# A decoder layer on one core: self-attention scores in two 64-row halves, a new order of TensorE's work, and gathers moved back in the first stage

## The chip, the cores and the metric

One core of a Trainium2 chip runs the whole program, with full-precision (f32) data. The metric is the time of one execution in microseconds (us) on the device. Engines: TensorE (PE; its weight loads are listed as PEld), VectorE (DVE), ScalarE (ACT), GpSimd (POOL) and SyncE (SP), which issues most DMAs.

## What is computed

`x` has 32 sequences of 64 tokens, 512 wide. The layer adds a self-attention, a cross-attention and a linear layer with low-rank additions, each on the layer norm of `x`:

```python
x = x + self_attention(layernorm(x), w_q, w_k, w_v, w_o)          # 32 heads of 16
x = x + cross_attention(layernorm(x), ctx, ctx, positions, mask)   # 32 heads of 128, 8 key/value heads, rotary
x = x + linear_with_lora(layernorm(x))
# self-attention, per head: softmax(q @ k.T / 4) @ v
# keys of the cross-attention: k = ctx @ Wk, then k * cos[pos] + rotate_half(k) * sin[pos]
```

## The kernel before

Five stages follow each other, each with its own buffers and a barrier between them: keys and values of the cross-attention (`keys_and_values`), layer norm and self-attention values (`norm_and_values`), `self_attention`, `cross_attention`, `lora_linear`. In each stage every engine has its own list of instructions, written out by hand in program order; semaphores tie them together. A product of two f32 matrices is made of three fp32r matmuls over high and low parts (`product3`, lines 75 to 77: the first, second and third).

**Self-attention** runs 16 iterations `it`: 4 groups of 8 heads (128 of the 512 columns) by 4 blocks of 512 tokens (8 sequences). In each iteration TensorE projects q and k (`project`, 12 matmuls of 128x512 each), ScalarE spreads them out with zeroed heads (`spread_q` 2 copies, `spread_k` 4 copies, lines 415 and 423), and then 4 units of 2 sequences each go through `scores` (line 349; one f32 matmul a sequence over all 128 rows, 128 queries wide and 256 keys deep), `shift` on VectorE (maximum and subtraction, lines 476 and 479), `exponentials` on ScalarE (430), `invert` on VectorE (sum and reciprocal, 484 and 487), `normalise_p` on GpSimd (552), `turn` on TensorE (4 transposes, 358), `copy_turned` on ScalarE (435) and `mix` with the values (373; the output in four groups of 32 columns). The result of an iteration is split (`outputs_hi` 440, `outputs_lo` 491), multiplied by `w_o` (`output`, 6 matmuls for two tiles of tokens) and added to x (`add`, 509); the last group also collects norm statistics in `add` (line 122). `place_values` (501) lays out the values of the next iteration with 4 VectorE copies.

TensorE's order in unit n is: scores(n+2), mix(n-1), turn(n), and then one of project k, output, project q, output. The buffers of scores, probabilities and their sums are double.

**Keys and values** of the cross-attention: SP loads the context and `wv` chunk by chunk, then `wk`; GpSimd issues 16 gathers of table rows (line 674) as soon as the positions are there. TensorE first makes the 8 value tiles of block 0 one after the other, transposes the gathered rows into cosine and sine tables (814), and then makes the keys of block 0; blocks 1 to 3 alternate keys and values. Each key tile is rotated by three VectorE operations into `ra` and `rb` (563 to 565), which GpSimd adds into `k_out` (681), and SP stores that. `rotate` of a tile waits for the addition of the tile before it, since `ra` and `rb` are single. `keys` of a tile waits until the tile two before it has been rotated.

Of the kernel before, what the change touches and what calls it, by code (L numbers as in the profile page):

```python
# [26 lines left out]
P = 128  # L27
# [12 lines left out]
QSETS, KSETS = 2, 4  # L40
# [217 lines left out]
def self_attention(nc, stack_type, x, norm2, xt_hi, xt_lo, v1, ident, wq_dram, wk_dram, wo_dram, heads_dram):  # L258

    with stack_type() as stack:  # L260
# [3 lines left out]
        UNITS, UB = 4, BLOCK // SEQ // 4  # L264
        UNITS_ALL = ITS * UNITS
        BB = BLOCK // SEQ
        raw = {w: m.sb(f"raw_{w}", [P, KC, P]) for w in "qk"}
# [4 lines left out]
        heads = m.sb("heads", [P, QSETS + KSETS])  # L272
        q_x = [m.sb(f"q_x{i}", [P, BB, QSETS, SEQ]) for i in range(2)]
        k_x = [m.sb(f"k_x{i}", [P, BB, KSETS, SEQ]) for i in range(2)]
# [3 lines left out]
        pn = [m.sb(f"pn{i}", [P, UB * KSETS, SEQ]) for i in range(2)]  # L278
        pt = [m.sb(f"pt{i}", [P, UB * KSETS // 2, P]) for i in range(2)]
        mx = [m.sb(f"mx{i}", [P, UB * KSETS]) for i in range(2)]  # L280
        total = [m.sb(f"total{i}", [P, UB * KSETS]) for i in range(2)]
        inv = [m.sb(f"inv{i}", [P, UB * KSETS]) for i in range(2)]
        o_hi, o_lo = m.sb("o_hi", [P, BLOCK], F32R), m.sb("o_lo", [P, BLOCK], F32R)
        ps_in = {w: m.ps(f"ps_{w}") for w in "qk"}
        ps_o, ps_p = m.ps("ps_o"), m.ps("ps_p")
        ps_s = [m.ps(f"ps_s{i}") for i in range(2)]
# [9 lines left out]
        v_ready, pv_done, out_hi, out_lo, y_done, y_added = (m.sem(n) for n in ("v_ready", "pv_done", "out_hi", "out_lo", "y_done", "y_added"))  # L296

        block = stack.enter_context(nc.Block())

# [3 lines left out]
        def block_of(it):  # L303
            return it % NB

# [26 lines left out]
        def _(pe):  # L332
            def project(w, it):

                need(pe, ready[w], group_of(it) + 1)
                need(pe, {"q": q_spread, "k": k_spread}[w], it)
                tokens = slice(block_of(it) * BLOCK, (block_of(it) + 1) * BLOCK)
                product3(nc, ps_in[w][:, :], [(w_hi[w][:, c, :], w_lo[w][:, c, :], xt_hi[:, c, tokens], xt_lo[:, c, tokens])
                                           for c in range(KC)]).then_inc(done[w], 1)

            def scores(n):

                it, u = n // UNITS, n % UNITS
# [3 lines left out]
                for r in range(UB):  # L347
                    b = u * UB + r
                    mm = nc.tensor.matmul(ps_s[n % 2][:, r * KSETS * SEQ:(r + 1) * KSETS * SEQ],
                                          q_x[it % 2][:, b, :, :].rearrange("p e q -> p (e q)"),  # L350
                                          k_x[it % 2][:, b, :, :].rearrange("p j k -> p (j k)"), start=True, stop=True)
                mm.then_inc(s_done, 1)

            def turn(n):
                need(pe, p_norm, n + 1)
                need(pe, pt_copied, n)
                for i in range(UB * KSETS // 2):
                    tr = nc.tensor.transpose(ps_p[:, i * P:(i + 1) * P], pn[n % 2][:, 2 * i:2 * i + 2, :].rearrange("p j k -> p (j k)"),
                                             ident[:, :])
                tr.then_inc(p_turned, 1)  # L360

            def mix(n):

                it, u = n // UNITS, n % UNITS
                need(pe, pt_copied, n + 1)
                if u == 0:
                    need(pe, v_ready, it + 1)
                    need(pe, out_lo, it)
                for r in range(UB):
                    b = u * UB + r  # L370
                    for c in range(HPG1 // 2):
                        half, e = c % (KSETS // 2), c // (KSETS // 2)
                        mm = nc.tensor.matmul(ps_o[c * 2 * D1:(c + 1) * 2 * D1, b * SEQ:(b + 1) * SEQ], v_x[it % 2][:, b, c, :],
                                              pt[n % 2][:, r * KSETS // 2 + half, e * SEQ:(e + 1) * SEQ], start=True, stop=True)
                mm.then_inc(pv_done, 1)

            def output(it, pair):
                need(pe, out_lo, it + 1)
                need(pe, ready["o"], group_of(it) + 1)
                need(pe, y_added, it * 2 + pair)  # L380
                for t in (2 * pair, 2 * pair + 1):
                    product3(nc, ps_y[:, t % 2, :], [(o_hi[:, t * P:(t + 1) * P], o_lo[:, t * P:(t + 1) * P],
                                                      wo_hi[:, :], wo_lo[:, :])]).then_inc(y_done, 1)
# [4 lines left out]
            scores(0)  # L388
            scores(1)
            for n in range(UNITS_ALL):  # L390
                it, u = n // UNITS, n % UNITS
                if n + 2 < UNITS_ALL:
                    scores(n + 2)
                if n > 0:
                    mix(n - 1)
                turn(n)
                if u == 0 and it + 1 < ITS:
                    project("k", it + 1)
                if u == 1 and it > 0:
                    output(it - 1, 0)  # L400
                if u == 2 and it + 2 < ITS:
                    project("q", it + 2)
                if u == 3 and it > 0:
                    output(it - 1, 1)
            mix(UNITS_ALL - 1)
            output(ITS - 1, 0)
            output(ITS - 1, 1)

        @block.scalar
        def _(act):  # L410
            def spread_q(it):
                need(act, done["q"], it + 1)
                need(act, s_done, (it - 1) * UNITS)
                for e in range(QSETS):
                    c = nc.scalar.activation(q_x[it % 2][:, :, e, :], ps_in["q"][:, :].rearrange("p (b q) -> p b q", q=SEQ), ACT.Copy,
# [3 lines left out]
            def spread_k(it):  # L419
                need(act, done["k"], it + 1)  # L420
                need(act, s_done, (it - 1) * UNITS)
                for j in range(KSETS):
                    c = nc.scalar.activation(k_x[it % 2][:, :, j, :], ps_in["k"][:, :].rearrange("p (b q) -> p b q", q=SEQ), ACT.Copy,
                                             scale=heads[:, QSETS + j:QSETS + j + 1])
                c.then_inc(k_spread, 1)

            def exponentials(n):
                need(act, s_shifted, n + 1)
                need(act, p_norm, n - 1)
                nc.scalar.activation(p[n % 2][:, :, :], s[n % 2][:, :, :], ACT.Exp, scale=SCALE).then_inc(p_exp, 1)  # L430

            def copy_turned(n):
                need(act, p_turned, n + 1)
                need(act, pv_done, n - 1)
                nc.scalar.activation(pt[n % 2].rearrange("p i q -> p (i q)"), ps_p[:, :], ACT.Copy).then_inc(pt_copied, 1)

            def outputs_hi(it):
                need(act, pv_done, (it + 1) * UNITS)
# [10 lines left out]
            exponentials(0)  # L449
            exponentials(1)  # L450
            for n in range(UNITS_ALL):
                it, u = n // UNITS, n % UNITS
                if u == 1 and it + 1 < ITS:
                    spread_k(it + 1)
                if u == 3 and it + 2 < ITS:
                    spread_q(it + 2)
                if u == 0 and it > 0:
                    outputs_hi(it - 1)
                copy_turned(n)
                if n + 2 < UNITS_ALL:  # L460
                    exponentials(n + 2)
                if block_of(it) == NB - 3 and u == 3 and group_of(it) + 1 < G1:
                    split_hi(act, "q", group_of(it) + 1, done["q"], it + 3)
# [1102 lines left out]
```

## Time and profile before

| | |
|---|---|
| median of 3 runs | 1610.09 us (1608.79 to 1610.84) |
| the profiled execution's own time | 1609.72 us |
| its span, first to last instruction | 1607.8 us |
| busy, share of the span | PE 93%, PEld 74%, DVE 70%, ACT 29%, POOL 30% |
| mean granted TensorE clock | 0.972 |
| `keys_and_values` | 0 to about 209 us |
| `norm_and_values` | about 209 to 271 us |
| `self_attention` | about 271 to 552 us |
| `cross_attention` and `lora_linear` | from 552 us |

A row of the timeline gives the start, the duration from the first start to the last end, the engine, the line, the operation with its tiles, how many instructions were merged, and in brackets the idle time before it and what ended it.
### The profile page before, as it was taken

To read this page: it belongs to the slowest core of one execution; us is meant where nothing else is said; L and a number is where in the kernel's file an instruction comes from. 1 tells how busy PE (TensorE), PEld (TensorE's weight loads), DVE (VectorE), ACT (ScalarE), POOL (GpSimd) and SP (SyncE) were. 2 spreads that over 40 slices of the span, in tenths; PEclk is the share of its full clock that TensorE was granted. 3 is DMA by queue.
4 is the path that set the end of the run, shared out by engine and by line. 5 is a ranking of instruction groups with operands and counts; after the bars stand their busy time and mean duration, and the time that the engine had idled before them with its cause. 6 is when DMAs were issued, how large, how long until landed. Compare 5 with 4: busy or idle time off the path is not lost. (4 is left out here: it accounts for less than half of the span.)

```text
span 1607.8 us, 25367 instructions
## 1 busy us (share of the span) xinstructions
PE 1502.7 (93%) x9824; PEld 1192.1 (74%) x9824; DVE 1132.3 (70%) x1819; ACT 458.3 (29%) x802; POOL 481.1 (30%) x411
## 2 busy tenths in 40 slices
PE   7899978999999569999999999999999999998698
PEld 5688856677777357787778878877877787786476
DVE  3555333688888677787887787787887877886454
ACT  4111133565555221222221221222222212211311
POOL 4322212222222123332432423433333324231022
PEclk9999989999999779999999999999999999999799
DMA  7455211000000221001020110020020201000211
GB/s 231 134 180 171 100 51 39 1 14 21 8 2 1 87 72 52 27 21 60 27 66 14 40 53 27 28 66 22 19 66 27 61 19 40 14 27 1 89 46 59
DMA packets 79107, 83.89 MB, mean 52 GB/s; under 512 B 9824, under 2 KB 50928, under 8 KB 78736
## 3 DMA queue, kind: packets, MB, share of 16 engines
q1 hardware_dynamic: 68976, 63.42, 12.4%
q10 hardware_dynamic: 9216, 16.78, 3.2%
q0 software_dynamic: 800, 2.11, 0.4%
q8 instruction: 78, 1.28, 0.3%
q14 instruction: 37, 0.30, 0.1%
HBM read 59.22 MB, written 23.07 MB: 51 GB/s over the span
## 5 line engine op out<-in xcount | busy, mean ns | idle before, releaser
L1211 POOL TENSOR_TENSOR p_q_rot<-p_ra,p_rb 128x512 f32<-128x512 f32 x128 | 166.9, 1304 | 286.7 <-DVE p_rb L565 286.7
L981 PE MATMUL p_ps_y<-p_wo_hi,p_o_hi 128*128 128x512 f32 x512 | 212.8, 416 | 5.6 <-DVE p_o_lo L1130 5.4
L75 PE MATMUL p_ps_q<-b_xt_hi,p_wq_hi 128*128 128x512 f32 x512 | 211.3, 413 | 0.0
L982 PE MATMUL p_ps_y<-p_wo_lo,p_o_hi 128*128 128x512 f32 x512 | 203.2, 397 | 0.0
L983 PE MATMUL p_ps_y<-p_wo_hi,p_o_lo 128*128 128x512 f32 x512 | 203.0, 396 | 0.0
L76 PE MATMUL p_ps_q<-b_xt_lo,p_wq_hi 128*128 128x512 f32 x512 | 202.4, 395 | 0.0
L77 PE MATMUL p_ps_q<-b_xt_hi,p_wq_lo 128*128 128x512 f32 x512 | 201.2, 393 | 0.0
L1203 POOL TENSOR_TENSOR p_pn<-p_p,p_inv 128x512 f32<-128x512 f32 x64 | 66.8, 1043 | 298.2 <-DVE p_inv L1110 298.2
L1052 ACT ACTIVATE p_o_hi<-p_ps_o 128x512 fp32r<-128x512 f32 x128 | 69.5, 595 | 281.0 <-PE p_ps_o L968 281.0
L1140 DVE TENSOR_TENSOR x_sb<-p_ps_y,x_sb 128x512 f32<-128x512 f32 x128 | 88.0, 688 | 87.3 <-PE p_ps_y L983 87.3
L563 DVE TENSOR_TENSOR p_ra<-p_ps_q,b_cos_t 128x512 f32<-128x512 f32 x128 | 85.9, 671 | 59.8 <-PE p_ps_q L77 56.4
L552 POOL TENSOR_TENSOR p_pn<-p_p,p_inv 128x512 f32<-128x512 f32 x64 | 66.7, 1043 | 196.1 <-DVE p_inv L487 196.1
L981 PEld LDWEIGHTS p_ps_y<-p_wo_hi,p_o_hi 128*128 128x128 f32 x512 | 96.6, 189 | 30.4 <-DVE p_o_lo L1130 9.6
L75 PEld LDWEIGHTS p_ps_q<-b_xt_hi,p_wq_hi 128*128 128x128 f32 x512 | 97.5, 190 | 27.6
L983 PEld LDWEIGHTS p_ps_y<-p_wo_hi,p_o_lo 128*128 128x128 f32 x512 | 96.7, 189 | 23.2
L77 PEld LDWEIGHTS p_ps_q<-b_xt_hi,p_wq_lo 128*128 128x128 f32 x512 | 97.1, 190 | 22.3
L982 PEld LDWEIGHTS p_ps_y<-p_wo_lo,p_o_hi 128*128 128x128 f32 x512 | 97.1, 190 | 18.6
L76 PEld LDWEIGHTS p_ps_q<-b_xt_lo,p_wq_hi 128*128 128x128 f32 x512 | 97.5, 190 | 18.0
L1039 ACT ACTIVATE p_p<-p_s 128x512 f32<-128x512 f32 x64 | 40.5, 633 | 202.2 <-DVE p_s L1102 202.2
L1044 ACT ACTIVATE p_pt_hi<-p_ps_p 128x512 fp32r<-128x512 f32 x64 | 38.2, 598 | 192.2 <-PE p_ps_p L953 192.2
L564 DVE TENSOR_TENSOR p_rb<-p_ps_q,b_sin_t 64x512 f32<-64x512 f32 x128 | 88.7, 693 | 1.7
L565 DVE TENSOR_TENSOR p_rb<-p_ps_q,b_sin_t 64x512 f32<-64x512 f32 x128 | 87.5, 684 | 1.7
(179 smaller groups left out, 3163.2 us busy)
## 6 DMA issues: line engine op xcount, KB each, us to landing
p_raw_q<-in_wq SPq DMA_DIRECT2D x36, 256.0 KB, 3.2
v_scratch<-p_v_out SPq DMA_DIRECT2D x32, 256.0 KB, 2.7
k_scratch<-p_k_out SPq DMA_DIRECT2D x32, 256.0 KB, 2.1
p_k_t<-k_scratch ACTq DMA_DIRECT2D x32, 256.0 KB, 2.6
p_v_in<-v_scratch ACTq DMA_DIRECT2D x32, 256.0 KB, 2.8
p_raw_o<-in_wo SPq DMA_DIRECT2D x32, 256.0 KB, 3.6
x_sb<-in_x SPq DMA_DIRECT2D x16, 256.0 KB, 3.1
out<-p_yb SPq DMA_DIRECT2D x16, 256.0 KB, 2.0
```

The source lines that it names most:

```text
L75: nc.tensor.matmul(out, lh, rh, start=(c == 0), stop=False)
L76: nc.tensor.matmul(out, lh, rl, start=False, stop=False)
L77: mm = nc.tensor.matmul(out, ll, rh, start=False, stop=(c == last))
L563: nc.vector.tensor_tensor(a[:, :], ps[:, :], cos, ALU.mult)
L564: nc.vector.tensor_tensor(b[0:HALF, :], ps[HALF:D2, :], sin[HALF:D2], ALU.mult)
L565: return nc.vector.tensor_tensor(b[HALF:D2, :], ps[0:HALF, :], sin[0:HALF], ALU.mult)
L981: nc.tensor.matmul(ps_y[t][:, :], oh, w_hi["o"][h][:, :], start=(h == 0), stop=False)
L982: nc.tensor.matmul(ps_y[t][:, :], oh, w_lo["o"][h][:, :], start=False, stop=False)
L983: mm = nc.tensor.matmul(ps_y[t][:, :], ol, w_hi["o"][h][:, :], start=False, stop=(h == H - 1))
L1052: nc.scalar.activation(o_hi[:, :, :, r, :], ps_o[r][:, :].rearrange("p (t h q) -> p t h q", t=UT, h=H), ACT.Copy).then_inc(out_hi, 1)
L1140: nc.vector.tensor_tensor(x[:, tile + t, :], ps_y[t][:, :], x[:, tile + t, :], ALU.add).then_inc(y_added, 1)
L1211: nc.gpsimd.tensor_tensor(q_rot[:, h, :], ra[:, :], rb[:, :], ALU.add).then_inc(q_added, 1)
```

## The change

In self-attention the heads are laid out so that the upper and the lower 64 rows hold 4 heads each, with 2 sets of queries and 2 of keys in either half. A sequence then takes two matmuls of 64 rows, 128 queries and 128 keys, which write two banks, instead of one of 128 rows, 128 queries and 256 keys. `spread_k` makes 2 copies instead of 4. Units are twice as large (4 sequences, 2 an iteration); transposing, copying and mixing still go by 2 sequences, as parts. The softmax buffers `s`, `p`, `mx`, `total`, `inv` and the scores' banks become single; the transposes get two banks, and q and k share one bank (`ps_qk`) from iteration 2 on. TensorE's order in unit n becomes: mix of two parts, turn of two parts, scores(n+2), project k or q two iterations ahead, and two tiles of output. Half of the value layout moves from VectorE to GpSimd, and VectorE's additions move to the front of its unit.

In the first stage GpSimd waits for all 8 chunks of `wv` before it issues its 16 gathers; the first 4 value tiles are accumulated chunk by chunk as the chunks arrive; `rb` is double and the first term of the rotation goes straight into `k_out`, so that a rotation waits for the addition two before it and for the store of the buffer.

```diff
@@ self_attention: buffers and TensorE
-QSETS, KSETS = 2, 4
+SETS = 2
-        UNITS, UB = 4, BLOCK // SEQ // 4
+        UNITS, UB = 2, BB // 2
+        PARTS, PB = 4, BB // 4
-        s = [m.sb(f"s{i}", [P, UB * KSETS, SEQ]) for i in range(2)]
-        p = [m.sb(f"p{i}", [P, UB * KSETS, SEQ]) for i in range(2)]
+        s, p = m.sb("s", [P, COLS, SEQ]), m.sb("p", [P, COLS, SEQ])
-        ps_o, ps_p = m.ps("ps_o"), m.ps("ps_p")
-        ps_s = [m.ps(f"ps_s{i}") for i in range(2)]
+        ps_qk, ps_o = m.ps("ps_qk"), m.ps("ps_o")
+        ps_p = [m.ps(f"ps_p{i}") for i in range(2)]
+        ps_s = m.ps("ps_s", (P, ROWS, UB * SETS * SEQ))
+        def projection_bank(w, it):
+            return ps_p[1] if w == "k" and it < 2 else ps_qk
@@ project
-                need(pe, {"q": q_spread, "k": k_spread}[w], it)
+                if it < 2:
+                    need(pe, {"q": q_spread, "k": k_spread}[w], it)
+                elif w == "k":
+                    need(pe, q_spread, it)
+                else:
+                    need(pe, k_spread, it + 1)
@@ scores
-                need(pe, s_shifted, n - 1)
+                need(pe, s_shifted, n)
+                for b in range(UB):
+                    for r in range(ROWS):
+                        rows = slice(r * SPAN, (r + 1) * SPAN)
+                        mm = nc.tensor.matmul(ps_s[:, r, b * SETS * SEQ:(b + 1) * SETS * SEQ],
+                                              q_x[it % 2][rows, first + b, :, :].rearrange("p e q -> p (e q)"),
+                                              k_x[it % 2][rows, first + b, :, :].rearrange("p m k -> p (m k)"), start=True, stop=True)
@@ TensorE's order
             scores(0)
+            project("k", 1)
             scores(1)
-                if n + 2 < UNITS_ALL:
-                    scores(n + 2)
-                if n > 0:
-                    mix(n - 1)
-                turn(n)
-                if u == 0 and it + 1 < ITS:
-                    project("k", it + 1)
-                if u == 1 and it > 0:
-                    output(it - 1, 0)
-                if u == 2 and it + 2 < ITS:
-                    project("q", it + 2)
-                if u == 3 and it > 0:
-                    output(it - 1, 1)
+                if n > 0:
+                    mix(2 * n - 2)
+                    mix(2 * n - 1)
+                turn(2 * n)
+                turn(2 * n + 1)
+                if n + 2 < UNITS_ALL:
+                    scores(n + 2)
+                if it + 2 < ITS:
+                    project("kq"[w], it + 2)
+                if it > 0:
+                    output(it - 1, 2 * w)
+                    output(it - 1, 2 * w + 1)
@@ ScalarE's order in unit n: outputs_hi (w 0), copy_turned twice, then
+                if n + 2 < UNITS_ALL:
                     exponentials(n + 2)
+                if it + 2 < ITS:
+                    if w == 0:
+                        spread_k(it + 2)
+                    else:
+                        spread_q(it + 2)
@@ exponentials
-                need(act, p_norm, n - 1)
+                need(act, p_norm, n * 2)
@@ VectorE's order in unit n
+                if w == 0 and it > 1:
+                    add(it - 2, 1)
+                if w == 1 and it > 0:
+                    add(it - 1, 0)
+                if w == 0 and it > 0:
+                    outputs_lo(it - 1)
                 if n + 1 < UNITS_ALL:
                     invert(n + 1)
                 if n + 2 < UNITS_ALL:
                     shift(n + 2)
+                if w == 1 and it + 1 < ITS:
+                    move_values(it + 1)
@@ GpSimd's order
+            for n in range(1, UNITS_ALL):
+                normalise_p(2 * n)
+                normalise_p(2 * n + 1)
+                if n % UNITS == 1 and n // UNITS + 1 < ITS:
+                    place_values(n // UNITS + 1)
@@ keys_and_values
+            for n in range(NH * KC):
+                pool.wait_ge(v_raw_in[n], 16)
             for t in range(TILES):
                 pool.indirect_dma_start(rows[:, t, :], None, table_dram, ...)
-                need(dve, k_added, n)
-                rotate_terms(nc, ps_k[i % 2], ..., ra, rb).then_inc(k_terms, 1)
+                need(dve, k_added, n - 1)
+                need(dve, k_stored[i % 2], (b * (KVH // 2) + i // 2) * 16)
+                rotate_terms(nc, ps_k[i % 2], ..., k_out[i % 2], rb[i % 2]).then_inc(k_terms, 1)
+            def first_values():
+                for c in range(KC):
+                    pe.wait_ge(c_ready, c + 1)
+                    pe.wait_ge(ready["v"], c + 1)
+                    for i in range(TPB):
+                        out, tile = values_bank(0, i)[:, :], slice(i * P, (i + 1) * P)
...
+                        nc.tensor.matmul(out, ch, wh, start=(c == 0), stop=False)
+                        nc.tensor.matmul(out, ch, wl, start=False, stop=False)
+                        mm = nc.tensor.matmul(out, cl, wh, start=False, stop=(c == KC - 1))
```

## Rows read from the trace of the kernel before

**Rows 1.** Windows, thirteen iterations: length, PE, PEld, DVE, ACT, POOL busy; clock, DMA share, GB/s.
```profile
306.48:513.32 206.84, 206.84 (x1755) 160.82 (x1753) 172.76 (x316) 122.76 (x209) 55.29 (x53) 1.00 0.03 9
```

**Rows 2.** Timeline of TensorE over two units of one iteration.
```profile
399.85 1.02 PE L349 MATMUL p_ps_s<-p_k_x,p_q_x 128*128 128x256 f32 x4
400.80 0.43 PE L373 MATMUL p_ps_o<-p_pt,p_v_x 128*32 128x64 f32 x16
401.16 0.66 PE L358 MATMUL p_ps_p<-ident,p_pn 128*128 128x128 f32 x4
401.57 0.48 PE L75 MATMUL p_ps_k<-a_xt_hi,p_wk_hi 128*128 128x512 f32 x1
...
404.41 1.03 PE L349 MATMUL p_ps_s<-p_k_x,p_q_x 128*128 128x256 f32 x4
...
407.63 1.02 PE L349 MATMUL p_ps_s<-p_k_x,p_q_x 128*128 128x256 f32 x4
```

**Rows 3.** Timeline of TensorE at the start of self-attention.
```profile
292.46 0.66 PE L358 MATMUL p_ps_p<-ident,p_pn 128*128 128x128 f32 x4 [2.08 <-POOL p_pn L552]
...
306.48 1.03 PE L349 MATMUL p_ps_s<-p_k_x,p_q_x 128*128 128x256 f32 x4
```

**Rows 4.** Timeline of TensorE and VectorE at the end of self-attention.
```profile
508.75 1.02 PE L349 MATMUL p_ps_s<-p_k_x,p_q_x 128*128 128x256 f32 x4
...
539.93 0.43 PE L373 MATMUL p_ps_o<-p_pt,p_v_x 128*32 128x64 f32 x16
...
550.50 1.29 DVE L122 BATCH_NORM_STATS2 stats<-x_sb 128x6 f32<-128x512 f32 x2
```

**Rows 5.** Keys of block 0: a rotation, an addition, and the store's median landing time.
```profile
49.95 1.78 POOL L681 TENSOR_TENSOR p_k_out<-p_ra,p_rb 128x512 f32<-128x512 f32 x1 [23.78 <-DVE p_rb L565]
51.84 0.69 DVE L563 TENSOR_TENSOR p_ra<-p_ps_k,p_cos_t 128x512 f32<-128x512 f32 x1 [1.25 <-POOL p_k_out L681]
...
k_scratch<-p_k_out SPq DMA_DIRECT2D x3, 256.0 KB, 2.0
```

**Rows 6.** Timeline of the first stage: ScalarE, GpSimd and TensorE.
```profile
15.46 0.63 ACT L693 ACTIVATE p_wv_hi<-p_raw_v 128x512 fp32r<-128x512 f32 x1 [0.43 <-DMA p_raw_v<-in_wv]
...
25.22 0.95 POOL L674 DMA_INDIRECT p_rows<-in_table_c,p_pos  x1 [0.30 <-issue]
...
39.21 1.03 PE L814 MATMUL p_ps_r<-ident,p_rows 128*128 128x128 f32 x8
...
44.65 0.47 PE L75 MATMUL p_ps_k<-p_c_hi,p_wk_hi 128*128 128x512 f32 x1
...
76.19 0.39 PE L75 MATMUL p_ps_v<-p_wv_hi,p_c_hi 128*128 128x512 f32 x1
```

**Rows 7.** Groups by line, 0 to 650 us: count | busy, mean ns | idle before.
```profile
L552 POOL TENSOR_TENSOR p_pn<-p_p,p_inv 128x512 f32<-128x512 f32 x64 | 66.7, 1043 | 196.1 <-DVE p_inv L487 196.1
L349 PE MATMUL p_ps_s<-p_k_x,p_q_x 128*128 128x256 f32 x256 | 66.6, 383 | 1.5 <-issue 0.7 <-DVE p_s L479 0.7
...
L349 PEld LDWEIGHTS p_ps_s<-p_k_x,p_q_x 128*128 128x128 f32 x256 | 48.4, 192 | 11.3 <-issue 2.8
...
L476 DVE TENSOR_REDUCE p_mx<-p_ps_s 128x8 f32<-128x512 f32 x64 | 42.4, 662 | 18.7 <-PE p_ps_s L349 18.7
L430 ACT ACTIVATE p_p<-p_s 128x512 f32<-128x512 f32 x64 | 40.6, 634 | 43.8 <-DVE p_s L479 43.5
L509 DVE TENSOR_TENSOR x_sb<-p_ps_y,x_sb 128x1024 f32<-128x1024 f32 x32 | 38.8, 1213 | 5.8 <-PE p_ps_y L77 5.8
```

**Rows 8.** Timeline of TensorE in cross-attention, matmuls on half the columns or rows.
```profile
708.98 1.15 PE L943 MATMUL p_ps_s<-p_k_t,p_q_rot 128*64 128x64 f32 x32
710.06 0.39 PE L968 MATMUL p_ps_o<-p_pt_hi,p_v_hi 64*128 64x256 f32 x2
...
710.97 0.50 PE L75 MATMUL p_ps_q<-b_xt_hi,p_wq_hi 128*128 128x512 f32 x1
```

**Rows 9.** Windows, columns as in rows 1, from the first transpose of self-attention on.
```profile
292.50:297.30 4.80, 4.80 (x17) 3.84 (x17) 1.71 (x4) 1.11 (x2) 1.94 (x2) 0.64 0.02 3
```

More of the change, by code:

```diff
@@ L339, in project @@
                                            for c in range(KC)]).then_inc(done[w], 1)
             def scores(n):
-                it, u = n // UNITS, n % UNITS
+                it, first = n // UNITS, n % UNITS * UB
                 need(pe, q_spread, it + 1)
                 need(pe, k_spread, it + 1)
-                need(pe, s_shifted, n - 1)
[L347 to L351, printed above, removed]
@@ L359, in turn, with mix @@
+                mm.then_inc(s_done, 1)
+            def turn(j):
+                need(pe, p_norm, j + 1)
+                need(pe, pt_copied, j - 1)
+                need(pe, k_spread, 2)
+                for i in range(ROWS * PB):
+                    tr = nc.tensor.transpose(ps_p[j % 2][:, i * P:(i + 1) * P], pn[j % 2][:, 2 * i:2 * i + 2, :].rearrange("p m k -> p (m k)"),
                                              ident[:, :])
                 tr.then_inc(p_turned, 1)
-            def mix(n):
-                it, u = n // UNITS, n % UNITS
-                need(pe, pt_copied, n + 1)
+            def mix(j):
+                it, u = j // PARTS, j % PARTS
+                need(pe, pt_copied, j + 1)
@@ L366, in mix @@
                 if u == 0:
-                    need(pe, v_ready, it + 1)
+                    need(pe, v_placed, it + 1)
+                    need(pe, v_moved, it + 1)
                     need(pe, out_lo, it)
-                for r in range(UB):
-                    b = u * UB + r
+                for i in range(PB):
+                    b = u * PB + i
                     for c in range(HPG1 // 2):
-                        half, e = c % (KSETS // 2), c // (KSETS // 2)
+                        r, e = c // SETS, c % SETS
@@ L379, in output @@
                 need(pe, ready["o"], group_of(it) + 1)
[L380 to L383, printed above, removed]
+                need(pe, y_added, it * 2 + t // 2)
+                product3(nc, ps_y[:, t % 2, :], [(o_hi[:, t * P:(t + 1) * P], o_lo[:, t * P:(t + 1) * P],
+                                                  wo_hi[:, :], wo_lo[:, :])]).then_inc(y_done, 1)
@@ L517, in _ @@
             dve.wait_ge(zeroed, 2)
-            place_values(0)
+            move_values(0)
             shift(0)
@@ L589, in keys_and_values, with values_bank @@
         ps_v = [m.ps(f"ps_v{i}") for i in range(2)]
+        def values_bank(b, i):
+            return ps_k[i % 2] if b == 0 and 2 <= i < TPB else ps_v[i % 2]
         pos_in, id_in, row_in, row_turned, row_copied, tables_out = (
```

201 lines of the change are left out of this document (100 added, 101 removed).

## The prediction, made before the result was known

> **What bounds the kernel now.** The mean busy shares of the page say TensorE, but the change touches two stages, so I read those. First the busy times over the middle of self-attention: TensorE is busy in all 206.84 us, at a granted clock of 1.00, and VectorE in 172.76 [rows 1]. Then TensorE's own timeline: its four kinds of work follow each other with no idle time. Scores of a unit take 0.95 us, from 399.85 to 400.80, mixing 0.36, turning 0.41, and projecting k 2.84; a unit with output instead takes 3.22 in all, so output is 1.50 [rows 2]. Four units, two with a projection and two with output, make 2 x 4.56 + 2 x 3.22 = 15.56. The distance from 306.48 to 508.75 over thirteen iterations gives 15.56 as well [rows 3, 4]. So each us that leaves TensorE's list here leaves the time, until another engine is late. Before and after this stretch latency rules: a first transpose that comes at 292.46 after 2.08 idle [rows 3], and an end at 550.50 + 1.29 = 551.8 [rows 4]. In the first stage the keys of block 0 are bound by VectorE and GpSimd in turn: a rotation waits 1.25 for the addition of 1.78 [rows 5], and the eight key tiles and the first keys of block 1 take from 44.65 to 76.19, 31.5 us for nine tiles of 2.73 [rows 6].
>
> **Scores in two halves.** A unit of before has four passes (two for each f32 matmul) of 256 columns, (1.02 - 0.383) / 3 = 0.21 apart [rows 2, 7]. A unit of after covers twice the sequences and has 16 passes of 128 columns, 0.107 each by the same rate. If upper and lower half run side by side, that is 8 x 0.107 = 0.86; if one after the other, 1.71, what it costs now. Side by side is what cross-attention shows: six pairs of 64-row fp32r matmuls of 256 columns take 0.91 from 710.06 to 710.97, all switching included, where twelve in series would need 12 x 0.114 = 1.37 (an fp32r matmul of 512 columns costs (2.84 - 0.1) / 12 = 0.228 [rows 2]). Two f32 passes of one tile in a row are no obstacle with column halves either: 32 passes of 64 columns take 1.08, and in series 32 x 0.053 = 1.71 [rows 8]. I take 0.91 + 2 x 0.107 = 1.12 for eight pairs with both switches.
>
> **The rest of TensorE's unit.** Mixing twice: 0.36, and the second without a switch; between 0.36 and 0.72 I take 0.57. Turning twice 0.82. One more switch behind the turning and one ahead of the mixing, 0.1 each, which is what scores cost above their four passes (0.95 - 4 x 0.21) [rows 2]. Projection 2.84. Output follows a projection of the same kind, so 0.1 less: 1.40. Sum 6.95 a unit, 13.9 an iteration; bounds 13.5 (second mixing and switches free) and 14.5 (all switches doubled). Over thirteen full iterations 13 x 1.66 = **21.6** less.
> The page TensorEngine Tiling (Array Packing) of the Trainium skill, Tiling Modes, Key Properties, speaks against the change here: switching the tiling mode drains the array. The trace agrees in kind, with about 0.1 a switch; before there are three changes of shape in each quarter iteration and after four in each half, so by that rule too the sum gets smaller and not larger.
>
> **Do the others keep up?** VectorE in an iteration: a pass over 512 columns costs 0.66, over 1024 columns 1.21 [rows 7]. Twice (sum, reciprocal 0.2, maximum, subtraction) = 7.7, two additions 2.4, output's low part 0.7, half of the value copies 0.6: 11.4, with weights some 11.9, against 13.9. The single buffers form loops. Scores(n+1) end, maximum and subtraction 2.4, exponentials 1.06 (0.63 for 512 columns [rows 7], twice that less the fixed part), spreading q in two copies 1.3, then scores(n+2), which need that q: 5.1 with the hand-overs, where TensorE has 5.8 of projection, output, mixing and turning in between. That leaves 0.7. ScalarE's spread stands behind exponentials in its queue, those behind the subtraction, and this behind the addition and the inversion on VectorE; in the unit with the low part the subtraction ends about 6.3 after the unit's start and the spread of k at 8.8, where project q wants it at 9.7. GpSimd: two halves of the normalisation at 1.04, and two copies, against 6.9 a unit; its normalisation ends well before the next turning. The probabilities' loop, invert 1.4, normalise 2.1, exponentials 1.06, is 4.9. So none is late in the steady part, by a narrow margin.
>
> **Start and end of the stage.** The first transpose needs, on VectorE, two shifts of 2.4 ahead of the first inversion. The first scores end near 287.7 by TensorE's order, project k(1) takes 2.84 more, and the second scores start at 290.5. So 290.5 + 1.0 + 2.4 + 1.4 + 1.04 and hand-overs = 296.7 against 292.46 [rows 3], with TensorE idle for 5. After such a gap the granted clock falls: it was 0.64 from 292.50 to 297.30 [rows 9]. From there to iteration 1 I count 12.4, against 14.0 before (part of it works off what is already projected), so 2.6 later, and 0.7 once for a spread that is late there: **3.3 more**. At the end no projections remain, and VectorE sets the pace with norm statistics of 1.29: two units of 7.0 [rows 4, 7]. Then add 2.5, low part 0.7, invert 1.4, normalise 2.1, turning, output and mixing 3.8, which is 10.5, and the output's end 551.8 - 539.93 = 11.9 as now. That is 36.4 from iteration 14's start, against 551.8 - 508.75 = 43.0 [rows 4]: **6.6 less**. Half an iteration more was scored by then.
>
> **First stage.** With two buffers, a rotation waits for the store of the tile two before: rotation 2.1 (three of 0.69), addition 1.8 [rows 5], store 2.0, hand-overs 0.3, which is 6.2 for two tiles, or 3.1 each, and not 2.73. Now the next rotation starts only behind the addition, with 0.69 of context work between: 2.1 + 1.8 + 0.2 = 4.1 each [rows 5]. Through the seven rotations that the first keys of block 1 wait for, I get 26.2 for the stretch that takes 31.5: **5.0 less**, bounds 3.5 and 6.9 (TensorE alone). Blocks 1 to 3 are full of matmuls and change nothing. Gathers: the last ends at 25.22 + 0.95; 16 take 1.25 each. The last chunk of `wv` was there at 15.46 [rows 6] with some eight gathers beside the loads; without them I take 12.8, an estimate. Gathers then end at 33 and the last row lands at 35.5; the values are done before, at 30 (96 matmuls at 0.228 from about 6.4 on, the first ten at half the clock), since the first chunk alone gives TensorE 12 matmuls. The tables' transposes take 5.4, from 39.21 to 44.65 [rows 6], so keys start at 41 in place of 44.65, less 1.5 for a clock that fell meanwhile: **2.2 less**. Bounds: 2 more (`wv` no earlier, rows landing 5 us after issue) and 4 less.
>
> **Sum.** 21.6 - 3.3 + 6.6 + 5.0 + 2.2 = 32.1. From the profiled execution's 1609.7 that is 1577.6. The runs' median is 0.4 above that execution, so this is within the rounding: **1577.5**. Own range with the bounds of the parts: 1567 to 1587.
>
> **The rivals.**
> Halves in series. The f32 halves might not overlap, since the rows show full-precision overlap only for column halves and row halves only for fp32r. Then a unit costs 0.86 more, 26 units 22: 1600.
> A late queue. The margins of 0.7 and 0.9 are thinner than my errors in six durations. If TensorE waits 0.7 in each unit, that is 18: 1595. For it speaks that the buffers are single; against it that VectorE has 15% to spare.
> Weight loads in the open, on the other side. Each pass of scores has a load of its own, and loads of this shape take 0.192 [rows 7], while a pass of 128 columns streams for 0.107. If loads are not hidden, 16 passes cost 3.1 and not 0.86, 2.2 more a unit, 57 in all: 1635. It turns the change into a loss once a pass costs over 0.13 on average, for 16 x (0.13 - 0.053) x 26 = 32. Against it stands that the four passes of before are 0.21 apart with a load of 0.192 each, on the same rows, which leaves no room for an exposed one, and the pairs of cross-attention. If only the second pass of each matmul is held up by its load, behind the first on the same rows, that is eight loads in the open, 8 x (0.192 - 0.053) = 1.1 a unit, 29 in all: 1606.
> The page TensorE: Matmul & The Clock Gate of the Trainium skill, Part 3, The mechanism, says that a weight load overlaps with running matmuls only when the row group differs. By that rule the second of these cases would come, 1606; the 0.21 between passes on the same rows disagrees.
> Nothing gained in the first stage (late rows, a cold clock): 1585, in my own range.
>
> **How the numbers follow.** The forecast 0.62 (the empty first stage in it), the late queue 0.16, halves in series 0.10, half of the loads in the open 0.04, all of them 0.05 (slower); 0.03 is left for something that cancels the gain. The range 1567 to 1600 leaves out the loads in the open and little else. Faster by over 0.2%, about what a measurement of this kernel can tell from no change: 0.91; within it 0.03; slower 0.06, since the last two cases can spill over.
>
> **What would show it.** In TensorE's timeline a unit of 6.9 to 7.0, scores as 16 passes in about 1.1, VectorE some 82% busy, no waits of scores or projections on the spreads. In the first stage keys starting near 41 to 42 and rotations about 3.1 apart. Scores of 1.9 a unit would show series; 3 and more, exposed loads; idle time of TensorE ahead of scores or project q, with ScalarE's spread as what ended it, the late queue.

## The result, and the profile after

| | before | after |
|---|---|---|
| median | 1609.9 us (4 runs) | 1587.15 us (1584.68 to 1588.91, 4 runs) |
| the profiled execution's own time, its span | 1609.72, 1607.8 | 1588.91, 1587.1 |
| busy, share of the span | PE 93%, DVE 70%, ACT 29%, POOL 30% | PE 93%, DVE 70%, ACT 27%, POOL 31% |
| start of self-attention (first projection) | 276.48 | 272.82 |
| end of self-attention (last statistics) | 551.8 | 531.6 |

The ratio is 0.986, with an interval of 0.984 to 0.987. The forecast was 1577.5: 32.1 us less were worked out, and 22.8 less came out. The measured time lies inside the stated range of 1567 to 1600.

TensorE's timeline over one unit of the changed kernel, against [rows 2] (start, duration from first start to last end, engine, line, tiles, count; in brackets the idle time before it and what ended that):

```profile
345.74 1.16 PE L366 MATMUL p_ps_s<-p_k_x,p_q_x 64*128 64x128 f32 x16
346.83 0.50 PE L75 MATMUL p_ps_qk<-a_xt_hi,p_wq_hi 128*128 128x512 f32 x1
...
351.19 0.65 PE L392 MATMUL p_ps_o<-p_pt,p_v_x 128*32 128x64 f32 x32
351.78 1.09 PE L376 MATMUL p_ps_p<-ident,p_pn 128*128 128x128 f32 x8
352.80 1.16 PE L366 MATMUL p_ps_s<-p_k_x,p_q_x 64*128 64x128 f32 x16
```

The 16 passes of the scores are followed by a projection 1.09 later, the mixing by the turning 0.59 later, and the next scores start at 352.80: a unit is 7.06, without idle time. But the units are not all like this. The same timeline where the weights of the next group are prepared, with VectorE's and ScalarE's rows:

```profile
329.48 1.16 PE L366 MATMUL p_ps_s<-p_k_x,p_q_x 64*128 64x128 f32 x16
330.16 0.63 ACT L332 ACTIVATE p_wq_hi<-p_raw_q 128x512 fp32r<-128x512 f32 x1
330.82 0.69 DVE L339 TENSOR_TENSOR p_wq_lo<-p_raw_q,p_wq_hi 128x512 fp32r<-128x512 f32 x1 [2.79 <-ACT p_wq_hi L332]
331.56 0.50 PE L75 MATMUL p_ps_qk<-a_xt_hi,p_wq_hi 128*128 128x512 f32 x1 [0.92 <-DVE p_wq_lo L339]
332.56 1.21 DVE L507 TENSOR_REDUCE p_total<-p_p 128x16 f32<-128x1024 f32 x1
...
338.69 1.16 PE L366 MATMUL p_ps_s<-p_k_x,p_q_x 64*128 64x128 f32 x16 [1.10 <-ACT p_q_x L434]
```

Here scores are 9.21 apart (338.69 - 329.48), and again at 397.32 and 455.94: three borders between groups of heads, 2.15 too much at each. VectorE has nothing to do for 2.79 and yet can't go on: its low part waits for the high part, which stands in ScalarE's queue behind exponentials and a spread. All that VectorE has behind it (the addition, the inversion, the next shift) is late then, and the next scores wait. TensorE is idle twice for it: 0.92 ahead of the projection of q, which needs the low part itself, and 1.10 ahead of the scores, for a spread of q that comes late. One unit earlier VectorE waits 2.18 for the low part of k. That unit is still 7.06 long, but its subtraction starts 4.4 behind the scores (326.80 - 322.42), and 3.6 in the same unit of another iteration, so the exponentials and what stands behind them in ScalarE's queue begin 0.8 late. The waits of this stretch, from 306 to 510 (who waited for whom, us in total, times, longest):

```profile
DVE x_sb L528 <- PE p_ps_y L77: 16.5, 16, 1.4
...
DVE p_wq_lo L339 <- ACT p_wq_hi L332: 8.4, 3, 2.8
DVE p_wk_lo L339 <- ACT p_wk_hi L332: 6.5, 3, 2.2
```

Before the change the high part had one of the smaller units as a head start in the two lists, and no low part waited:

```profile
321.89 0.61 ACT L321 ACTIVATE p_wq_hi<-p_raw_q 128x512 fp32r<-128x512 f32 x1
...
327.19 0.68 DVE L328 TENSOR_TENSOR p_wq_lo<-p_raw_q,p_wq_hi 128x512 fp32r<-128x512 f32 x1
```

In the changed kernel both parts of a split stand at the end of the same unit, one in ScalarE's list and one in VectorE's. The windows view with its columns as in [rows 1], over six plain units:

```profile
345.74:388.10 42.36, 42.36 (x445) 33.70 (x444) 33.29 (x40) 21.39 (x35) 14.95 (x18) 1.00 0.03 8
```

VectorE is 79% busy. By busy time alone no engine but TensorE binds, so the borders look like a matter of queues; the run with earlier splits tests this.

The first stage, against [rows 6]: ScalarE's copies of value tiles and tables, GpSimd's last gather and TensorE.

```profile
28.04 0.60 ACT L747 ACTIVATE p_v_out<-p_ps_v 128x512 f32<-128x512 f32 x1
...
37.17 0.60 ACT L747 ACTIVATE p_v_out<-p_ps_v 128x512 f32<-128x512 f32 x1 [8.02 <-remote]
...
33.59 0.95 POOL L719 DMA_INDIRECT p_rows<-in_table_c,p_pos  x1 [0.30 <-issue]
...
36.46 1.06 PE L869 MATMUL p_ps_r<-ident,p_rows 128*128 128x128 f32 x8 [1.66 <-DMA p_rows<-in_table_c,p_pos]
39.83 5.55 PE L869 MATMUL p_ps_r<-ident,p_rows 128*128 128x128 f32 x24 [2.31 <-ACT p_cos_t L762]
...
45.05 0.55 PE L75 MATMUL p_ps_k<-p_c_hi,p_wk_hi 128*128 128x512 f32 x1
...
71.19 0.39 PE L75 MATMUL p_ps_v<-p_wv_hi,p_c_hi 128*128 128x512 f32 x1
```

Keys start at 45.05 (before 44.65), and the values of block 1 come 26.14 later (before 31.54). The copy at 37.17 waited 8.02, by its place in the program for the store of the tile two before it; the first copy of a table stands behind it, and TensorE's second part of the table waits 2.31 for that. The granted clock from 39.83 to 45.05 was 0.50; before the change it was 1.00 over the same transposes.

### The profile page after: what moved, and what is told of

Same layout as the page of the kernel before. It is cut to its first block and busy times, and to the rows that moved or that the text cites. A ratio compares the mean times of both kernels' runs of the same rounds, so it can differ in the third digit from the quotient of the medians.

```text
span 1587.1 us, 25598 instructions
## 1 busy us (share of the span) xinstructions
PE 1477.8 (93%) x10080; PEld 1179.6 (74%) x10080; DVE 1110.4 (70%) x1659; ACT 428.2 (27%) x738; POOL 493.6 (31%) x443
```

## The experiments

Their interval is that of the ratio to the kernel before on the same chip; its medians there were 1610.0 to 1610.5.

**One row half.** Both halves of the scores read rows 0 to 63, so the scores of the upper heads are left out.

```diff
-                        rows = slice(r * SPAN, (r + 1) * SPAN)
+                        rows = slice(0, SPAN)
```

> The changed kernel, but both halves of the scores are computed from rows 0 to 63: all instructions, sizes and waits stay, only the upper half of the array is not used, and the scores of the upper heads are those of the lower (this part of the computation is replaced). Theory (the two row halves run side by side and the whole steady gain is theirs): 16 passes of 128 columns in series take 16 x 0.107 + 0.2 = 1.9 instead of 1.09 a unit, 0.82 more, over 29 full units 24: 1611, the time of the kernel before, so that the new order of TensorE's work alone is worth nothing. Rival (half of the gain is the order, with fewer switches between shapes): scores do not run side by side, they take 1.1 here too, and the time stays at 1587. Rival (loads of weights in the open, once they are all for the same rows): 16 x 0.192 = 3.1 a unit, 2.0 more, 58 in all: 1645.

Measured: 1611.47 us, 24.3 above the changed kernel, ratio 1.0006 (0.9996 to 1.0017). TensorE's timeline of it, with the loads of weights (PEld):

```profile
397.25 1.86 PEld L366 LDWEIGHTS p_ps_s<-p_k_x,p_q_x 64*128 64x128 f32 x16 [0.17 <-issue]
397.25 2.05 PE L366 MATMUL p_ps_s<-p_k_x,p_q_x 64*128 64x128 f32 x16
399.23 0.50 PE L75 MATMUL p_ps_qk<-a_xt_hi,p_wq_hi 128*128 128x512 f32 x1
```

The passes take 1.98 instead of 1.09 and the units are 7.95 apart. So the two row halves do run side by side in f32, and this is the whole steady gain: half an iteration of before is 7.78, and the new order with halves in series would be 0.17 slower than that. The 16 loads, of 0.188 each and all for the same rows, are not in the open either: a pass is 0.124 (1.98 / 16), less than a load.

**Splits earlier.** ScalarE's high parts of the next group's weights move ahead of the exponentials, VectorE's low parts between the inversion and the shift.

```diff
+                if w == 1 and b == NB - 3 and g + 1 < G1:
+                    split_hi(act, "k", g + 1, done["k"], it + 3)
+                if w == 0 and b == NB - 2 and g + 1 < G1:
+                    split_hi(act, "q", g + 1, done["q"], it + 2)
                 if n + 2 < UNITS_ALL:
                     exponentials(n + 2)
...
-                if w == 1 and b == NB - 3 and g + 1 < G1:
-                    split_hi(act, "k", g + 1, done["k"], it + 3)
-                if w == 0 and b == NB - 2 and g + 1 < G1:
-                    split_hi(act, "q", g + 1, done["q"], it + 2)
...
+                if w == 1 and b == NB - 3 and g + 1 < G1:
+                    split_lo(dve, "k", g + 1)
+                if w == 0 and b == NB - 2 and g + 1 < G1:
+                    split_lo(dve, "q", g + 1)
                 if n + 2 < UNITS_ALL:
                     shift(n + 2)
...
-                if w == 1 and b == NB - 3 and g + 1 < G1:
-                    split_lo(dve, "k", g + 1)
-                if w == 0 and b == NB - 2 and g + 1 < G1:
-                    split_lo(dve, "q", g + 1)
```

> The changed kernel, with the splitting of the next group's weights moved up in its iteration: ScalarE's high part ahead of the exponentials, VectorE's low part between the inversion and the shift. Theory (VectorE is held up behind the split): in the trace of the changed kernel the scores are 9.2 us apart instead of 7.06 once at each of the three group borders, and there VectorE waits 2.8 for a high part that stands in ScalarE's queue behind exponentials and a spread. With the split moved up these 3 x 2.15 = 6.5 us go, less about 0.5 for work that now stands ahead of a shift: 1581, 6 less than the changed kernel, and the scores at the borders are at most 7.6 apart. Rival (the border's delay is the work itself, a busy VectorE or ScalarE that has to do 1.3 to 2 us more in that unit): the delay moves with the split and the time stays within 2 of 1587. Rival on the other side: the high part now stands ahead of exponentials that the next inversion waits for, each border costs 1 more than now, and the time is 1590.

Measured: 1581.93 us, ratio 0.983 (0.981 to 0.985), 5.2 below the changed kernel. The border in its timeline:

```profile
319.52 1.16 PE L366 MATMUL p_ps_s<-p_k_x,p_q_x 64*128 64x128 f32 x16 [0.42 <-ACT p_q_x L434]
...
320.79 0.66 ACT L332 ACTIVATE p_wq_hi<-p_raw_q 128x512 fp32r<-128x512 f32 x1
...
322.01 0.63 DVE L339 TENSOR_TENSOR p_wq_lo<-p_raw_q,p_wq_hi 128x512 fp32r<-128x512 f32 x1
```

The low part of q waits for nothing now. Scores are 7.55 apart once per border (319.52, 376.49 and 433.46) instead of 9.21, so 3 x 1.66 = 5.0 of the 6.5 are back. The same work on the same engines, in another place of two queues: the stall was the order, not the load. The splits of k and of q were moved together, so the share of each isn't measured. The 0.49 that is left at a border stands behind the low part of k, which still waits 0.36 to 0.63 for its high part and now precedes a shift.

**Self-attention alone**, with the first stage of the kernel before (`keys_and_values` taken from it whole).

> The changed kernel's self-attention with the first stage of the kernel before: neither the late gathers nor the rotation that adds in place. The traces put the start of self-attention 3.7 us earlier in the changed kernel. Theory (the two parts simply add): the time is 1587.2 + 3.7 = 1591, so self-attention alone gives 19 of the 22.8. Rival (the first stage's gain is lost in the start of self-attention, where weights and tables have to be there): 1587 to 1588.

Measured: 1592.48 us, ratio 0.989 (0.987 to 0.991). Self-attention alone gives 18.0 (1610.52 on its chip less 1592.48). What is left of the 22.8 for the first stage is 4.8; the plain difference of the two kernels is 5.3. The rival, that the first stage's gain is lost later, is out.

**Rotation alone**, in the kernel before.

```diff
-        ra, rb = m.sb("ra", [P, BLOCK]), m.sb("rb", [P, BLOCK])
+        rb = [m.sb(f"rb{i}", [P, BLOCK]) for i in range(2)]
...
-                    nc.gpsimd.tensor_tensor(k_out[i % 2][:, :], ra[:, :], rb[:, :], ALU.add)
+                    nc.gpsimd.tensor_tensor(k_out[i % 2][:, :], k_out[i % 2][:, :], rb[i % 2][:, :], ALU.add)
...
-                need(dve, k_added, n)
+                need(dve, k_added, n - 1)
+                need(dve, k_stored[i % 2], (b * (KVH // 2) + i // 2) * 16)
```

> The kernel before with one edit of the first stage: GpSimd adds in place, in the tile that is stored, and the tile of the sine products has two buffers, so that VectorE waits for the addition of the tile two before and for that tile's store. Theory (rotations come 3.05 apart on average in place of 4.07 for the tiles of block 0, and nothing else of the first stage has to change for it): from the first keys to the first values of block 1 it takes 26.1 instead of 31.5, 5.4 less, and the time is 1610 - 5.4 = 1604.7. Rival (the gain needs the new first values and the late gathers ahead of it, or it is given back at the start of self-attention): 1608 to 1610.

Measured: 1605.78 us, ratio 0.9972 (0.996 to 0.9984), 4.3 below before. Keys start at 44.68 in its trace and the values of block 1 at 70.73: 26.05, the 5.4 of the theory. About one of them is given back between there and self-attention (271.94 - 70.73 = 201.2 to the start of self-attention, before 276.48 - 76.19 = 200.3).

**Gathers at the start.** GpSimd no longer waits for the chunks of `wv`.

```diff
-            for n in range(NH * KC):
-                pool.wait_ge(v_raw_in[n], 16)
```

> The changed kernel, with the sixteen gathers issued at the start, as in the kernel before, and not behind the last chunk of wv; all else as changed. Theory (late gathers gave nothing, since the last of them lands when TensorE has long been ready and they delay the stores of the values): keys then start some 1 to 2 us earlier than the 45.2 of the changed kernel, and the time is 1585 to 1586. Rival (the early gathers hold up the loads of the weights, as the prediction had it): the last chunk of wv comes at 15.5 instead of 14, the values end 1 to 2 later, and the time is 1587 to 1589.

Measured: 1584.2 us, ratio 0.984 (0.982 to 0.985), 2.9 below the changed kernel. Keys start at 42.77, TensorE's first matmul at 6.45 where it was 6.50, and neither trace shows idle time between the first values' chunks. So the early gathers hold up no chunk of `wv` that TensorE waits for, and the late place of the gathers was no gain. That it was a loss this run alone can't tell: the intervals of the two kernels overlap. TensorE does wait here, at 28.87, 3.65 for the copy of a value tile, and the longest wait of such a copy for a store is 4.95.

**One gather.** Fifteen of the sixteen are left out, and GpSimd sets their rows to a constant.

> The changed kernel with one of its sixteen gathers; the other rows are set to a constant by GpSimd, so that the cosines and sines of all but the first 128 tokens are left out. Theory (the late store is the gathers' doing): without them no value copy waits more than 4 for a store, no transpose waits for rows, keys start at 42.5 or earlier, and the time is 1584. Rival (stores are late by themselves, from the loads of context and weights): a wait of 8 for a store is still there, keys start at 45, and the time is 1587.

Measured: 1579.07 us (2 runs), ratio 0.981 (0.979 to 0.983). The longest wait for a store is 2.74, keys start at 37.01. So the gathers, where the changed kernel has them, cost 8. The expectation had the direction, but had thought of the late store alone, worth 3. The runs with three buffers, below, show the rest.

**Both edits**, splits and gathers early, on one kernel.

> The changed kernel with both edits: the weight splits moved up, and the gathers issued at the start. Theory (the two add, since they sit in different stages): 1581.9 - 2.9 = 1579. Rival (late and early gathers are worth the same once no store of the values is late, as three of the four traces with late gathers have it, with keys starting at 42.5 to 43.0 and at 42.8 with early ones): 1581 to 1582.

Measured: 1581.0 us, ratio 0.982 (0.981 to 0.984): 2 above the sum of the two and within 0.9 of the splits alone, where the rival had it. The runs scatter from 1579.87 to 1584.39, so this one does not tell.

**First inversion ahead of the second shift**, with splits early; gathers late, and then early.

```diff
             shift(0)
+            invert(0)
             shift(1)
-            invert(0)
```

> The changed kernel with the weight splits moved up and, at the start of self-attention, VectorE's first inversion ahead of its second shift; the gathers stay late. Theory (the 5.19 us in which TensorE is idle ahead of its first transpose are VectorE's second shift of 2.4, which stands ahead of the first inversion and isn't needed by then): the first transpose comes 2.4 to 3 earlier, the second half of the start is then bound by the second inversion, which moves by about 1, and the time is 1580, 2 less than with the splits alone. Rival (what is won at the first transpose is lost at the third, which waits for the second unit's probabilities, in one buffer): 1582.

> The kernel with the weight splits moved up and the first inversion ahead of the second shift, with the gathers issued at the start. Against the one with late gathers on the same chip it shows what their place is worth. Theory (late gathers gain nothing and now and then make a store of the values land late): 1577, 2 to 3 less than with late gathers, with less scatter. Rival (their place is worth nothing): within 0.7 of the one with late gathers. Rival (the first loads come earlier with late gathers and this counts): 2 more than with late gathers.

Measured: 1580.27 us, ratio 0.981 (0.980 to 0.983), and 1577.17 us, ratio 0.979 (0.978 to 0.981). The first transpose of self-attention, in the changed kernel and then in the one with early gathers:

```profile
293.68 2.12 PE L376 MATMUL p_ps_p<-ident,p_pn 128*128 128x128 f32 x8 [5.19 <-POOL p_pn L575]
...
287.01 2.12 PE L376 MATMUL p_ps_p<-ident,p_pn 128*128 128x128 f32 x8 [2.37 <-POOL p_pn L575]
```

It comes 2.8 sooner after the first scores (7.57 instead of 10.39), and what follows keeps that: the scores of the fifth unit are 21.9 behind the first ones (301.31 and 279.44), in the changed kernel 25.0. Both edits without this one measured 1581.0 on the same chip, so with early gathers the inversion is worth 3.8. And on that chip late gathers cost 3.1. The trace with late gathers shows a wait of 8.09 of a value copy, like the 8.02 of the changed kernel's, with keys at 45.43; of the four traces with late gathers and two buffers, two have it, and the other two start keys at 42.49 and 42.95. The four with early gathers and the new first values (the last run's below among them) have no such wait.

**Three buffers for value tiles**, with late and with early gathers.

```diff
-        v_out = [m.sb(f"v_out{i}", [P, BLOCK]) for i in range(2)]
+        v_out = [m.sb(f"v_out{i}", [P, BLOCK]) for i in range(3)]
...
-                need(act, v_stored[i % 2], (b * (KVH // 2) + i // 2) * 16)
+                n = b * KVH + i
+                need(act, v_stored[n % 3], (n // 3) * 16)
```

> As the one with early splits, early inversion and late gathers (1580.3), with three buffers in place of two for value tiles on their way out, so that ScalarE's copy waits for the store of the tile three before. Theory (late gathers cost 3 us because in some executions one store of the values lands some 8 us late among them and the copy of the tile two after waits for it, and the copies of the tables behind that): with a third buffer TensorE's value matmuls go on, the keys start at 41.5 to 42.5 in every trace, and the time falls by 3 to 1577. Rival (the late rows themselves hold up the tables' transposes, by 1.4 to 2.3 in three traces): it stays at 1579 to 1580, with a wait of the transposes for the rows of 3 or more. Rival (it is no matter of stores; the loads of the first weights and of the context are what differs): no change, 1580.

> The best so far (1577.2: early splits, early inversion, early gathers) with three buffers for value tiles. Copies wait up to 4.95 for a store in the traces with early gathers and TensorE 3.65 for the copy. Theory: values end 1 to 1.5 earlier, the gathers' rows are there by 27, so keys start at 41 and the time is 1576. Rival (TensorE's idle time only moves from the values to the tables' transposes or to key weights, or the clock falls there): 1577.

Measured: 1582.28 us, ratio 0.983 (0.981 to 0.984), and 1574.18 us, ratio 0.978 (0.976 to 0.979). With late gathers it gained nothing, and the timeline says why:

```profile
30.88 0.60 ACT L749 ACTIVATE p_v_out<-p_ps_v 128x512 f32<-128x512 f32 x1 [1.60 <-PE p_ps_v L77]
...
35.10 0.95 POOL L720 DMA_INDIRECT p_rows<-in_table_c,p_pos  x1 [0.30 <-issue]
...
40.04 6.89 PE L871 MATMUL p_ps_r<-ident,p_rows 128*128 128x128 f32 x32 [9.20 <-DMA p_rows<-in_table_c,p_pos]
46.69 0.47 PE L75 MATMUL p_ps_k<-p_c_hi,p_wk_hi 128*128 128x512 f32 x1
```

The values are done by 31 and no copy is late, but the last gather is issued at 35.10 and its row is there at 40.0. TensorE is idle for 9.20, and the transposes take 6.65 (40.04 to 46.69) at a granted clock of 0.57, against 5.44 at 1.00 with early gathers. My theory of the late store fell here: with late gathers the rows are a floor at about 36 to 40 whatever happens to the stores, and the rival that I gave (a wait of 3 or more for the rows) came out, larger. What makes that floor differ by 3 between traces stays open. With early gathers the same buffer is worth 3.0 by the medians, of two chips:

```profile
34.16 1.03 PE L869 MATMUL p_ps_r<-ident,p_rows 128*128 128x128 f32 x8
...
39.60 0.47 PE L75 MATMUL p_ps_k<-p_c_hi,p_wk_hi 128*128 128x512 f32 x1
```

No wait for a row, and keys at 39.60, where they start at 42.32 with two buffers. This kernel, 1574.18 us, is faster than both: 36.2 below before and 13.0 below the changed one. It has all four edits: splits early, first inversion early, gathers at the start, and the third buffer. The two runs with three buffers differ in the place of the gathers alone, on one chip, and are 8.1 apart: this is the clearest measure of what late gathers cost.

## Why the prediction was right, and where it was off

The direction and the mechanism were right, the size was not: 32.1 was worked out and 22.8 came. By its own steps, in the profiled executions:

| step | worked out | came out |
|---|---|---|
| scores of a unit | 1.12 | 1.09 |
| unit | 6.95 | 7.06, and 9.21 three times |
| thirteen iterations | -21.6 | -11.9 |
| start | +3.3 | +3.5 |
| end | -6.6 | -8.1 |
| rotations to first values of block 1 | -5.0 | -5.4 |
| first values and gathers, to the first keys | -2.2 | +0.4 |

The mechanism forecast for self-attention came out. The number lies between the forecast and the rival of the late queue (1595), and 0.15 beyond the prediction's own range of 1567 to 1587. That range was too narrow for its parts: their pessimistic bounds (7.8 for the unit, 1.5 for the rotations, 4.2 for the first values) add up to 1591.

*Scores.* Right, and for the reason given: eight pairs side by side, loads hidden. The rival of halves in series had 1600 from 0.86 a unit; made to happen, it cost 0.89 a unit and 24 in all.

*The rest of the unit.* 7.06 against 6.95. Mixing 0.59 (0.57 taken), turning 1.02 with a switch (0.82 taken, and two switches of 0.1), projection 2.87, output 1.49 where 1.40 was taken. The 0.1 that output was to save behind a projection isn't there. Over 26 units 2.9.

*"None is late in the steady part".* This is the step that failed. In plain units it holds; the margins of 0.7 and 0.9 sufficed, no spread is late. At the borders between groups it fails, and the working shows how: the weights were entered only as busy time ("with weights some 11.9, against 13.9"). The prediction looked at what stands ahead of the spreads in ScalarE's queue, but not at what stands ahead of the two splits, which the change puts into one unit: before, the low part started 4.7 behind the end of its high part (322.50 and 327.19). VectorE's low part of q waits on ScalarE's high part, and that stands behind exponentials which wait on VectorE's shift. 3 x 2.15 = 6.5, of which the earlier splits returned 5.0. The rival "late queue" named the mechanism, but put it in every unit (18) and on the spreads.

*Start and end.* By distance from the first projection, iteration 1 begins 306.35 - 272.82 = 33.5 in, before 30.0. The idle time ahead of the first transpose was put at 5 and is 5.19. The end (from iteration 14's start at 496.69 to 531.6) takes 34.9 and not 36.4: the last two scores are 5.79 apart (498.33 and 504.12), where units of 7.0 were assumed. 11.9 - 3.5 + 8.1 is the 16.5 by which the stage is shorter.

*First stage.* The rotations are right: the stretch was worked out as 26.2 and is 26.14, with rotations 3.0 apart (seven from 48.26 to 69.35) for the expected 3.1. The 5.0 entered in the sum was a slip, since 31.5 - 26.2 is 5.3. First values and gathers are not right. The estimate that `wv` would arrive earlier without gathers beside it (12.8) was too hopeful (the first gather starts at 14.36). For the values this did not matter, because the new first values need only one chunk at a time; the chain of gathers ends at 34.5 instead of 33 for it. What mattered was that the last of sixteen gathers, 1.25 apart, lands at 36.5 to 40, when TensorE is done or nearly so. The working has keys at 42.4 (44.65 - 2.2), and they came at 45.05. The transposes start at 36.46, 1.0 behind the 35.5 of the working, and then take 8.6 where it has 6.9; the wait of 2.31 behind the late copy is in these 8.6. No row stood behind the 1.5 that the working took for a fallen clock; with three buffers and late gathers the transposes took 1.2 more at 0.57 than at 1.00. "The last row lands at 35.5" was the term on which the step hung, and the bound I gave it (rows 5 us after issue) is what the trace with three buffers shows. The new first values do gain about 2 (keys at 42.77 with early gathers, 44.68 with the old ones); late gathers take it away again in some executions. In the two traces with late gathers and no late copy keys start at 42.49 and 42.95, near the 42.4, but early gathers give as much.

The sum: the profiled execution is 20.8 faster, 11.3 less than worked out. The stretch of thirteen iterations accounts for 9.7 of that (2.9 for the unit, 6.5 for the borders, 0.3 for one late spread at its start), the first keys for 2.6, the start for 0.2; the end gives 1.5 back and the rotations 0.4. That is 10.6. The rest is 1.3 lost in blocks 1 to 3 of the first stage and the norm behind it, which take 201.6 (from 71.19 to 272.82) where they took 200.3, less 0.5 won behind self-attention (1055.5 for 1056.0). By the medians 9.3 remain: that of the changed kernel is 1.8 below this execution, and that of before 0.2 above its own. This execution has the late copy in it; whether that is the 1.8 is not shown.

The Trainium skill's rule in TensorE: Matmul & The Clock Gate, Part 3, The mechanism, that a weight load overlaps only with matmuls of another row group, is not borne out for these f32 passes: with all sixteen on one row half a pass takes 0.124 and a load 0.188. The same section also lets a load run ahead into a background weight buffer, which would fit; no run here can show such a buffer. The rival of half the loads in the open, 1606, did not come. The rule of TensorEngine Tiling (Array Packing), Tiling Modes, Key Properties, that a change of mode drains the array, agrees in kind, if the time lost at a change is that drain: the projection takes 2.87 where twelve matmuls 0.23 apart are 2.76, and scores take 1.09 where the passes alone were put at 0.86, so 0.1 to 0.2 a change.

## What to carry to other kernels

When work is moved between the queues of two engines, write down for each moved instruction what it waits for and what stands ahead of that in the other engine's queue: a busy share of 79% hid a stall of 2.8, and moving eight lines returned 5 us. Two f32 matmuls on 64 rows each, issued in turn, cost as one; that is worth a new layout of the operands where the contraction is half empty. Before delaying loads to make room for others, find the consumer of the last one: sixteen gathers in series are a chain of 20 us, and here an early start was worth 3 to 8 us, and a free channel nothing.

## What the hardware showed that I had not expected

Weight loads of 0.188 on the same 64 rows hid behind passes of 0.124, sixteen in a row: the sixteen loads took 1.86 from the first start to the last end, so that they overlap one another too. The last of sixteen indirect gathers landed 5 us after its issue in one trace (35.10 to 40.0), and in two of the four traces with late gathers and two buffers one value copy was held for 8.0 to 8.1; since the trace names no store there, that this is a late landing is read from the program's order and not shown. Leaving out fifteen gathers of 128 KB each was worth 8 us to a kernel in which TensorE is busy for 93% of the time.
